# Mamba step sizes in four column groups of the second y bank, and two projection tiles of the next sequence at other places in TensorE's order

## The reference

```
zxbcdt = X @ W_in.T                       # 512 -> 2*1024 (z, x) + 2*64 (B, C) + 16 (dt)
dt     = softplus(dt + dt_bias)           # a step size for each of the 16 heads
xBC    = silu(conv4(xBC) + conv_b)        # causal, 4 taps, over x (1024), B and C (64 each)
h_t    = h_{t-1} * exp(dt*A) + dt * B_t x_t ;  y_t = C_t h_t + D x_t
y      = y * silu(z); y = y * rsqrt(mean(y*y)) * norm_w ; out = y @ W_out.T
```

## Time and profile before

| what | us |
|---|---|
| median of three timed runs | 1930.55 (1924.72 to 1933.03) |
| the profiled execution, its own time | 1935.45 |
| its span in the trace | 1933.5 |
| PE busy | 1824.7 (94%) |
| DVE busy | 1430.8 (74%) |
| ACT busy | 1251.9 (65%) |
| POOL busy | 445.2 (23%) |

### The profile page before, as it was taken

One profiled execution on the slowest core, in us unless ns is written; L12 is line 12 of the kernel. 1 busy time (PEld: TensorE's weight loads), 2 busy tenths in 40 slices (PEclk: granted clock), 3 DMA queues, 4 the chain that ended last, 5 costly groups with the idle time before them and its releaser, 6 DMA issues. The chain is left out here.

```text
span 1933.5 us, 38723 instructions
## 1 busy us (share of the span) xinstructions
PE 1824.7 (94%) x12524; PEld 1288.2 (67%) x12524; DVE 1430.8 (74%) x3030; ACT 1251.9 (65%) x3128; POOL 445.2 (23%) x629
## 2 busy tenths in 40 slices
PE   7899999999999999789999999989999999899988
PEld 5677777777777777564666666656666663588853
DVE  8988888888888888647686868667777775566348
ACT  5646464646464645348989898878888886266614
POOL 1312121212121212421222121222232222100006
PEclk9999999999999999898999999989999996799999
DMA  7122131313131313433334343334343423721266
GB/s 235 53 55 96 50 101 49 102 48 103 50 102 48 103 47 104 137 97 93 105 90 122 91 117 102 111 106 116 100 121 92 125 68 103 228 92 47 75 210 257
DMA packets 123884, 200.60 MB, mean 104 GB/s; under 512 B 27184, under 2 KB 48688, under 8 KB 123440
## 3 DMA queue, kind: packets, MB, share of 16 engines
q1 hardware_dynamic: 114480, 179.20, 30.1%
q0 software_dynamic: 9216, 18.89, 3.9%
HBM read 117.27 MB, written 29.88 MB: 76 GB/s over the span
## 5 line engine op out<-in xcount | busy, mean ns | idle before, releaser
L1961 ACT ACTIVATE a_shared<-a_shared,a_mx 128x512 f32<-128x512 f32 x512 | 344.4, 676 | 57.7 <-DVE a_mx L2024 57.5
L2024 DVE TENSOR_REDUCE a_mx<-a_shared 128x1 f32<-128x512 f32 x512 | 328.3, 682 | 37.9 <-PE a_shared L2171 36.2
L1954 ACT ACTIVATE a_probs<-a_scores 128x512 f32<-128x512 f32 x512 | 302.8, 607 | 58.8 <-PE a_scores L2182 58.6
L2171 PE MATMUL a_shared<-a_ks,a_qs 96*128 96x512 f32 x512 | 213.7, 438 | 13.8 <-ACT a_shared L1961 8.5
L2182 PE MATMUL a_scores<-a_qs,a_ks 98*128 98x512 f32 x512 | 211.3, 427 | 9.8 <-DMA a_qs<-a_shift_rows 5.2
L2143 PE MATMUL a_shared<-link 128*128 128x512 f32 x768 | 201.7, 399 | 9.7 <-DVE a_v L2018 7.4
L1086 PE MATMUL m_proj<-m_xt_hi,link 128*128 128x512 f32 x448 | 182.2, 407 | 3.9 <-DVE m_acc L780 3.5
L2171 PEld LDWEIGHTS a_shared<-a_ks,a_qs 96*128 96x128 f32 x512 | 96.2, 194 | 132.9 <-ACT a_shared L1961 59.5
L600 ACT ACTIVATE m_xw<-m_added,m_wdt 128x64 f32<-128x64 f32 x256 | 55.8, 329 | 192.7 <-DVE m_xdt L868 192.7
L2143 PEld LDWEIGHTS a_shared<-link 128*128 128x128 f32 x768 | 146.6, 192 | 47.3 <-DVE a_v L2018 10.9
L1087 PE MATMUL m_proj<-m_xt_lo,link 128*128 128x512 f32 x448 | 176.5, 394 | 0.0
(11 more groups left out here) (305 smaller groups left out, 3828.2 us busy)
## 6 DMA issues: line engine op xcount, KB each, us to landing
m_dec<-step_decay SPq DMA_DIRECT2D x64, 256.0 KB, 4.1
a_qs<-link SPq DMA_DIRECT2D x256, 64.0 KB, 2.0
m_ce<-run_decay SPq DMA_DIRECT2D x128, 112.0 KB, 3.1
a_ks<-a_k_hi POOLq DMA_DIRECT2D x192, 64.0 KB, 2.4
e_x<-x SPq DMA_DIRECT2D x11, 1024.0 KB, 5.6
m_xt_in<-x_t_in SPq DMA_DIRECT2D x8, 1024.0 KB, 9.6
m_x_tok<-x_in SPq DMA_DIRECT2D x8, 1024.0 KB, 5.4
x<-m_x_tok SPq DMA_DIRECT2D x32, 256.0 KB, 2.8
```

The costliest lines, as they stand in the source:

```text
L1954: act.activation(probs[:, n % 2, h, :], scores[t.score_bank(n, h)][:, :], ACT.Exp, scale=-1.0).then_inc(exp_ready, 1)
L1961: act.activation(scored[:, :], scored[:, :], ACT.Exp, scale=-1.0, bias=mx[:, i % 2, j, h:h + 1], accum_out=den[:, i, j, h:h + 1]).then_inc ...
L2024: dve.tensor_reduce(mx[:, i % 2, j, h:h + 1], bank(what)[:, :], AX.X, ALU.min).then_inc(mx_ready, 1)
L2171: pe.matmul(bank(what)[:, :], qs[0:STACK, t.slot(i), h, j * P:(j + 1) * P], ks[0:STACK, t.slot(i), h, :], start=True, stop=True).then_inc( ...
```

## The change

Five things are altered, all in the Mamba stage.

1. `dt_proj` no longer uses the two parts of x. It takes `xt_in` as F32, with the same 32 weight columns read as F32, and makes four matmuls instead of eight: block k goes to partitions 32k to 32k+31 of one bank, so the four partial sums stand side by side instead of being added up in the bank. `turn_steps` adds them, by a matrix `group_sum` of 128 rows in place of `pair_sum` of 32; POOL builds it with four instructions instead of one.
2. The bank is `yp[1]` (called `raw_bank`, and `steps` for the turned ones) instead of `proj[0]`. So x tile 0 waits no longer for the step sizes' reading, and ACT's copy takes 128 rows instead of 32, after the whole split (it overwrites the first block of `xt_in`).
3. The next sequence's B-C tile stands ahead of the first added states of the last group, where the step sizes stood; the step sizes stand behind these added states.
4. x tile 0 stands ahead of the last group's carried outputs, where the B-C tile stood.
5. Of the output projection's first block, the first two matmuls stand between the carried outputs and x tile 1, and `decay_sums` goes two places later in it.

```diff
-        dt_ch = xt_in[0:2 * NH, 0, :]
+        dt_ch = xt_in[:, 0, :]
-        steps = proj[0]
+        raw_bank = steps = yp[1]
...
+            pool.wait_ge(const, SET - 1)
+            for k in range(KT):
+                rows = slice(k * 2 * NH, (k + 1) * 2 * NH)
+                ins = pool.tensor_tensor(group_sum[rows, :], ident[rows, 2 * k * NH:(2 * k + 1) * NH],
+                                         ident[rows, (2 * k + 1) * NH:2 * (k + 1) * NH], ALU.add)
...
             def raw_steps(b, first):
-                act.wait_ge(tile_done, at(b, 18, 1))
+                act.wait_ge(tile_done, at(b, 18, 1 if first else 2))
                 if not first:
                     act.wait_ge(dt_turned, at(b, 1, 0))
-                act.activation(dt_ch, proj[0][0:2 * NH, :], ACT.Copy).then_inc(dt_read, 1)
+                act.wait_ge(xt_split, at(b, KT, KT))
+                act.activation(dt_ch, raw_bank[:, :], ACT.Copy).then_inc(dt_read, 1)
...
                 elif n == 2:
-                    pe.wait_ge(dtv, at(b, DT_STEPS, 1))
+                    if not first:
+                        pe.wait_ge(z_ready, at(b, XT_TILES, 0))
...
                     wh, wl = win_hi[:, k, col:col + P], win_lo[:, k, col:col + P]
+                    if n == 1:
+                        pe.wait_ge(xt_split, at(b, KT, k + 1))
...
                 else:
-                    pe.wait_ge(z_ready, at(b, XT_TILES, 0))
+                    pe.wait_ge(y_read, at(b, XT_TILES, -2))
+                pe.wait_ge(xt_landed, at(b, 16, 16))
                 for k in range(KT):
-                    pe.wait_ge(xt_split, at(b, KT, k + 1))
-                    pe.matmul(proj[0][0:2 * NH, :], w_dt[:, k, :], xt_hi[:, k, :], start=(k == 0), stop=False)
-                    ins = pe.matmul(proj[0][0:2 * NH, :], w_dt[:, k, :], xt_lo[:, k, :], start=False,
-                                    stop=(k == KT - 1))
+                    ins = pe.matmul(raw_bank[k * 2 * NH:(k + 1) * 2 * NH, :], w_dt[:, k, :].bitcast(F32), xt_in[:, k, :],
+                                    start=True, stop=True)
...
-                    if t == 0 and n == 2 and more:
+                    if t == 0 and n == 4 and more:
                         decay_sums(b + 1, False)
...
                     if gr + 1 == NG and more:
+                        in_proj(b + 1, False, 1, COL_BC)
+                    added_states(b, gr, 0)
+                    if gr + 1 == NG and more:
                         dt_proj(b + 1, False)
-                    added_states(b, gr, 0)
                     local_outputs(b, first, gr, 1)
...
                         turn_steps(b + 1, False)
-                        in_proj(b + 1, False, 1, COL_BC)
+                        x_tile(b + 1, False, 0)
...
                 if more:
-                    for n in range(2):
-                        x_tile(b + 1, False, n)
-                out_proj(b, 0, more, range(0 if more else 2, XT_TILES))
+                    out_proj(b, 0, True, range(2))
+                    x_tile(b + 1, False, 1)
+                out_proj(b, 0, more, range(2, XT_TILES))
```

More of the change, by code:

```diff
@@ L145, in mamba_stage @@
         w_dt = sb("w_dt", [P, KT, 2 * NH], F32R)
-        pair_sum = sb("pair_sum", [2 * NH, NH])
+        group_sum = sb("group_sum", [P, NH])
         def over(name, tiles):
@@ L474, in _ @@
             ins.then_inc(const, 1)
-            pool.tensor_tensor(pair_sum[:, :], ident[0:2 * NH, 0:NH], ident[0:2 * NH, NH:2 * NH], ALU.add
-                               ).then_inc(const, 1)
+            pool.wait_ge(const, SET - 1)
[3 more added lines that the diff above has]
+                                         ident[rows, (2 * k + 1) * NH:2 * (k + 1) * NH], ALU.add)
+            ins.then_inc(const, 1)
             pool.wait_ge(const, SET)
@@ L1195, in turn_steps @@
                 for c in range(CH):
-                    ins = pe.matmul(steps[:, c * NH:(c + 1) * NH], dt_ch[:, c * P:(c + 1) * P], pair_sum[:, :],
+                    ins = pe.matmul(steps[:, c * NH:(c + 1) * NH], dt_ch[:, c * P:(c + 1) * P], group_sum[:, :],
                                     start=True, stop=True)
```

## The result

The change makes the kernel slower by a little: 1938.29 us (median of 20 runs, 1931.21 to 1943.68) against 1929.48 (20 runs, 1920.18 to 1933.40), ratio 1.0046 [1.0034, 1.0057]. The forecast was 1937.5 us, a ratio of 1.0036. The profiled execution took 1938.27 us, its span is 1936.2. The page's first part shows that the TensorE work did go away: PE was busy for 12.3 us less than in the earlier trace rows.

What follows compares the result with a forecast made beforehand. The junction path (weighted x, added states, DVE's unbroken 20.47 us, z tile 1) was the bound, not PE's total work; 6 x 1.0 + 1.8 - 7 x 0.1 - 0.2 = +6.9 us on 1930.55 gave 1937.5, range 1930 to 1946.

Steps and rivals of the forecast that it cites:

- The path: Junction between sequences: ACT's weighted x, PE's added states, 20.47 us of unbroken DVE work, then z tile 1 set the time.
- Rival A: PE is the bound after all, so 2.0 us come out at every junction: 14 us faster, 1917; chance 9%.
- The B-C tile in the shadow costs nothing: Ahead of the first added states, its 12 matmuls take 2.97 us while ACT makes weighted x: nothing won or lost.
- The step sizes at 1.0 us: Four column-group matmuls between first and second added states take 1.0 us, delaying states, DVE's run and z tile 1.
- Rival B: Step-size column groups don't overlap: 3.4 us each on the path, +23.7 us, 1954; chance 4%.
- Late low parts -0.1: DVE's last two low parts wait less for ACT's high parts: -0.1 us per junction.
- Its work from the states to the convolution keeps order and number: DVE's run in the junction passes the 1.0 us delay on; ACT's later raw copy is hidden by its idle time.
- First junction and head: First junction at half clock: +0.75 for the B-C tile plus 1.0 for step sizes, +1.8; program head -0.2 us.
- Rival C: PE's new waits within 14 us of the junction cost it the clock: +16 on top of 7, 1953; chance 3%.
- The waits forecast for PE: In the junction, PE's saved work turns up as waits of 0.8, 1, 0.7 and 0.6 us.
- lower sum: The total with step sizes at 0.86 us in place of 1.0: given as +5.8 us.

Runs made afterwards that it cites:

- e9: Kernel before, with VectorE's running decays and head weights moved behind the next sequence's second x convolution: 1926.45 us, ratio 0.9979.
- e1: Kernel before, with only the step sizes changed to four F32 matmuls in column groups, old bank and old place: 1946.14 us, ratio 1.0089.
- the tripled kernel: Kernel before, with step sizes in column groups (old bank, old place) and their four matmuls issued three times: 1936.76 us, ratio 1.0043.
- the late step sizes: Changed kernel, with the four step-size matmuls moved behind the second added states: 1943.96 us, ratio 1.0083 to the kernel before.
- e4: Kernel before, with column groups in old bank and place, and the last group's second local outputs ahead of its first added states: 1935.46 us, ratio 1.0041.
- e8: Kernel before, with column groups, half the B-C tile and second local outputs ahead of adjacent added states, ACT's squares early: 1929.85 us, ratio 0.9993.

## Why the prediction was right, and where it was not

1. **The path** (weighted x, added states, DVE's unbroken run, z tile 1) held in every junction behind the first: the idle time before the states went from 1.00 to 2.16, z tile 1 stayed 0.06 us behind the convolution, and the waits ahead of it took the work saved. Rival A (PE is the bound) fell: PE has 12.3 us less work and the time rose, and e9, with PE's work unchanged and the decays out of DVE's run ahead of z tile 1, got 0.65 us per period back.
2. **The B-C tile in the shadow costs nothing**: right, 2.99 us against 2.97, and no wait behind it. e1 shows what was not seen: something has to fill that shadow. Without it the clock falls.
3. **The step sizes at 1.0 us**: the four matmuls took 0.99, the number of the row, but the path grew by 1.15, inside the bounds of 0.86 and 1.25. The sum charged the matmuls alone. The 0.15 that their borders with the 64-wide tiles cost, six times over, it put at nothing, though it gave these borders as the reason for its upper bound. Twelve such matmuls as one group (the tripled kernel) take 2.78 us, 0.93 for four. The Trainium skill (TensorEngine Tiling (Array Packing), Key Properties) speaks of a drain at each change of tiling mode; the trace agrees in sign. The Trainium skill's ratio for three column tiles (TensorE: Matmul & The Clock Gate, Measured speedup vs the span model), 2.38, gives 1.08 us for three matmuls in the prediction, an estimate; the four took less here. Rival B needed 1.4 and didn't come.
4. **Late low parts -0.1**: right, -0.13.
5. **"Its work from the states to the convolution keeps order and number"**: true as it stands, and yet the step at which the sum failed. The order was kept, one duration was not: ACT's later raw copy was followed to the B-C tap on ACT alone, not to the squares behind it and POOL's sums behind these. That is +0.34 six times (0.24 at the first), 2.0 us, and with the late step sizes it was 2.15 each.
6. **First junction and head**: forecast 1.8 - 0.2, measured 1.85 for both. The parts differ: the twelve matmuls at half clock moved the added states by 0.71 (96.65 against 95.94), the step sizes cost 1.14, DVE's sizes in the head came 0.09 earlier, not 0.2.
7. **Rival C** (the new PE waits cost the clock) didn't come: waits of 1.11, 0.86, 0.39 and 0.36 us, clock 1.00. It was the right mechanism for another gap: e1 and e4 show it ahead of the added states.

Forecast +6.9 us; with items 3 and 5 measured (0.9 and 2.0) it is 9.8, as against 9.92 in the Mamba stage of the trace and 8.81 in the medians. The forecast of the difference was thus 1.9 us too low. That the median came out within 0.8 us of the forecast is in part luck: the sum started from a median of three runs, 1930.55, which over 20 runs is 1929.48. The waits forecast for PE (0.8, 1, 0.7, 0.6) add up to 3.1, those measured to 2.72. The prediction's lower sum is 5.9 by its own terms, not 5.8.

## What to carry to other kernels

Before moving work on a full engine, find what the end waits for: here a 94% busy TensorE was not the bound at the junction, and four matmuls that cost nothing in another engine's shadow cost 1.15 us each time when they stood between two halves of what that engine's follower needs. Follow a delayed instruction down its own queue and on to every engine behind it, POOL's too, and look which DVE instruction each of these will now stand beside. A shadow ahead of dependent matmuls should be filled with useful work: emptying it cost more than the work taken out.

## What the runs showed of the hardware

**Small DVE instructions blocked by POOL.** Instructions with 64 elements per partition took 1.22 and 1.36 us instead of 0.20 and 0.23 while POOL added two 128x512 tiles from SBUF; both times the hold ended where one of POOL's two sums did. In after, the state updates (one operand in PSUM) ran 2 us beside the same sums and kept 3.02 us for twelve, and L804, which reads PSUM, kept 0.22. The Trainium skill (SBUF — State Buffer, SBUF: two separate sides) calls the port pair that DVE and GpSimd share an exclusive lock for a whole instruction; the rows agree with it, L808 with two operands in SBUF, and show that L807 with one tensor operand is held up as well.

**Short idle times of TensorE can halve its clock.** Ahead of the added states 0.53 us (before) left it at 1.00, 1.41 us (e4) lost it in four of six junctions and 2.04 us (e1) in all six, which made these junctions 1.6 to 3.5 us longer. Four waits of 0.4 to 1.1 us between the projections' matmuls (after) lost nothing. These are the idle times of three kernels; how the clock is decided they don't show.

**A matmul group that waits for the one ahead of it** on the same engine started 0.81 us behind it in e8, with nothing in between: 0.65 us is the first group's own work, the rest is waiting. With the local outputs in between the states came only 0.1 us later (1.63 us from the first added states, 1.53 in e8).
